# Eight x buffers, beta added ahead on GpSimd, and single groups at the end of the output stage of an attention and expert layer

## The reference

```python
x = L0_attn_X                               # 8 x 512 x 256
xn = _layernorm(x, axis=-1)
# attention
P = softmax(Q1 K1^T * s) - lam * softmax(Q2 K2^T * s)
O = P V                                     # 16 heads of 64
Y = Ocat @ Wo + bo
Yn = (Y - mean(Y)) * rsqrt(var(Y) + 1e-5) * gamma + beta
attn = Yn * (1.0 - 0.8)
# experts: each row goes to the one with the highest route probability
y = gelu(t @ w1[e] + b1[e]) @ w2[e] + b2[e]
ffn = y * route_prob_max
return x + attn + ffn
```

## Time and profile before

| | |
|---|---|
| median of 3 runs | 1817.44 us (1816.18 to 1820.64) |
| the profiled execution's own time | 1819.72 us |
| its span in the profile | 1817.9 us |
| TensorE busy | 98% |
| VectorE, ScalarE, GpSimd busy | 85%, 78%, 35% |
| granted TensorE clock, mean over the span | 0.994 of full speed |

### The profile page before, as it was taken

The page is one execution under the profiler, slowest core; times in us unless marked ns, Lnnn a source line. Parts: engine busy times, 40 slices in busy tenths (PEclk is TensorE's granted clock), DMA queues, the critical chain, the costliest instruction groups (busy, mean ns, idle before and its releaser), DMA issues. The chain is left out here.

```text
span 1817.9 us, 33121 instructions
## 1 busy us (share of the span) xinstructions
PE 1777.5 (98%) x10714; PEld 1362.8 (75%) x10714; DVE 1542.1 (85%) x2636; ACT 1423.3 (78%) x3364; POOL 639.0 (35%) x711
## 2 busy tenths in 40 slices
PE   6999999999999999999999999999999999999997
PEld 5666667777777677777777677777777689999997
DVE  4988898898889988988898889888999866887667
ACT  4998888888888888888888888888888876677622
POOL 2443222322222222222322322322226546552255
PEclk8999999999999999999999999999999999999999
DMA  8998988898889888988898898888887676667797
GB/s 245 245 252 244 246 233 227 230 248 232 224 230 245 228 226 231 249 231 225 239 239 231 221 241 241 231 221 221 224 208 200 191 263 249 238 237 259 273 368 286
DMA packets 212120, 435.05 MB, mean 239 GB/s; under 512 B 29584, under 2 KB 107152, under 8 KB 203888
## 3 DMA queue, kind: packets, MB, share of 16 engines
q1 hardware_dynamic: 207104, 418.94, 82.7%
q0 software_dynamic: 4688, 13.51, 2.3%
q10 hardware_dynamic: 160, 0.52, 0.1%
HBM read 175.17 MB, written 49.15 MB: 123 GB/s over the span
## 5 line engine op out<-in xcount | busy, mean ns | idle before, releaser
L629 ACT ACTIVATE e<-p_score,nmax 128x512 f32<-128x512 f32 x1024 | 697.2, 688 | 123.3 <-DVE nmax L976 115.7
L976 DVE TENSOR_REDUCE nmax<-p_score 128x2 f32<-128x1024 f32 x512 | 623.1, 1217 | 149.9 <-PE p_score L1135 120.6
L493 POOL TENSOR_SCALAR e<-e,rrec,lam 128x512 f32<-128x512 f32 x512 | 394.0, 769 | 977.4 <-DVE rrec L943 977.0
L1135 PE MATMUL p_score<-ks,qs 128*128 128x512 f32 x1608 | 450.1, 402 | 10.4 <-DMA ks<-k_parts 8.2
L1089 PE MATMUL p_proj<-xh,w 128*128 128x512 f32 x1024 | 386.2, 418 | 6.6 <-DVE k_parts L918 5.2
L581 ACT COPY pT<-p_tr 128x512 f32<-128x512 f32 x512 | 302.9, 592 | 104.3 <-PE p_tr L1147 98.9
L950 DVE SCALAR_TENSOR_TENSOR pm<-e,rrec 128x512 f32<-128x512 f32 x512 | 383.2, 749 | 0.4 <-POOL e L493 0.2
L1135 PEld LDWEIGHTS p_score<-ks,qs 128*128 128x128 f32 x1608 | 292.4, 189 | 85.1 <-DMA ks<-k_parts 10.4
L1147 PEld LDWEIGHTS p_tr<-consts,pm 128*128 128x128 f32 x2048 | 241.7, 140 | 104.2 <-issue 39.6
L1147 PE MATMUL p_tr<-consts,pm 128*128 128x128 f32 x2048 | 315.1, 276 | 1.4 <-ACT pT L581 1.4
L1164 PE MATMUL p_pv<-pT,v 128*64 128x512 f32 x1024 | 247.8, 605 | 0.7 <-ACT pT L581 0.7
(11 more groups left out here) (219 smaller groups left out, 2029.8 us busy)
## 6 DMA issues: line engine op xcount, KB each, us to landing
ks<-k_parts SPq DMA_DIRECT2D x510, 256.0 KB, 5.0
qs<-q_parts SPq DMA_DIRECT2D x512, 128.0 KB, 4.7
w<-weight_parts_scratch SPq DMA_DIRECT2D x56, 1024.0 KB, 10.7
w<-in_w SPq DMA_DIRECT2D x46, 1024.0 KB, 7.3
oT_parts_scratch<-oT SPq DMA_DIRECT2D x32, 512.0 KB, 6.7
op<-oT_parts_scratch SPq DMA_DIRECT2D x16, 1024.0 KB, 9.4
wv<-weight_parts_scratch SPq DMA_DIRECT2D x56, 256.0 KB, 5.5
weight_parts_scratch<-w SPq DMA_DIRECT2D x8, 1024.0 KB, 5.8
```

The costliest lines, as they stand in the source:

```text
L493: nc.gpsimd.tensor_scalar(e2, e2, rrec[:, g % 4, 1:2], lam[:, 0:1], ALU.mult, ALU.mult).then_inc(s_e2, 1)
L629: nc.scalar.activation(ex[:, g % EX, m, :], p_score[g % 2][:, m, :], ACT.Exp, bias=nmax[:, g % 2, m:m + 1], accum_out=rsum[:, g % 4, m:m + ...
L976: vec.tensor_reduce(nmax[:, g % 2, :], p_score[g % 2][:, :, :], AXX, ALU.max, negate=True).then_inc(s_max, 1)
L1135: last_op = nc.tensor.matmul(p_score[g % 2][:, m, :], qs[j][u][:, m, qt * P:(qt + 1) * P], ks[j][u][:, m, part, :], start=(part == 0), sto ...
```

## The change

`RX = 8` buffers of x instead of 4. The four new ones lie in the place of `wo`, which is free after `s_wolo`. SP loads x of groups 4 to 7 into them in the expert stage, behind its bodies 14 to 17, and in the output stage x of group n + 6 where it loaded that of n + 2. GpSimd adds beta of groups 0 to 3 behind its subtraction of tiles 8 to 11, that of 4 to 7 behind the fetches of groups 0 to 3, and that of group n + 2 behind the fetch of group n for n from 6 to 13. The groups 12 to 15 have a turn of their own each. The semaphores `s_x` stay four; SP waits for `s_xb` (beta of group n - 4 is added) before it loads x of group n.

```diff
@@ -1288,8 +1288,9 @@
-        G, R, GROUPS = 2 * P, 4, T // (2 * P)
-        OUT_TURNS = [(n, n + 1) for n in range(0, GROUPS - 2, 2)] + [(GROUPS - 2,), (GROUPS - 1,)]
+        G, R, RX, GROUPS = 2 * P, 4, 8, T // (2 * P)
+        BETA_FROM, BETAS, MORE_FROM, LATE = 8, 4, 14, 6
+        OUT_TURNS = [(n, n + 1) for n in range(0, GROUPS - R, 2)] + [(n,) for n in range(GROUPS - R, GROUPS)]
@@ -1322,6 +1323,7 @@
         x = [sb(f"x{r}", [P, 2, E]) for r in range(R)]
+        x += [wo[:, 2 * r:2 * r + 2, :] for r in range(RX - R)]
@@ -1472,8 +1474,10 @@
             def load_x(n):
                 if n >= R:
-                    sp.wait_ge(s_out, 2 * (n - R) + 2)
-                sp.dma_start(x[n % R][:, :, :], x_v[n]).then_inc(s_x[n % R], 16)
+                    sp.wait_ge(s_xb, n - R + 1)
+                if n >= RX:
+                    sp.wait_ge(s_out, 2 * (n - RX) + 2)
+                sp.dma_start(x[n % RX][:, :, :], x_v[n]).then_inc(s_x[n % R], 16)
@@ -1499,7 +1503,13 @@
-            turns(body, before_last=first_o)(sp)
+            def more_x(n):
+                if n == MORE_FROM:
+                    sp.wait_ge(s_wolo, 2)
+                if 0 <= n - MORE_FROM < RX - R:
+                    load_x(n - MORE_FROM + R)
+
+            turns(body, before_last=first_o, after=more_x)(sp)
@@ -1515,8 +1525,8 @@
                 if n >= 2:
                     store_out(n - 2)
-                    if n - 2 + R < GROUPS:
-                        load_x(n - 2 + R)
+                    if n - 2 + RX < GROUPS:
+                        load_x(n - 2 + RX)
@@ -1543,36 +1570,19 @@
-            pool.wait_ge(s_scaled, 1)
-            pool.wait_ge(s_w2lo_dve, 1)
-            add_beta(0)
-            add_beta(1)
+                if n == BETA_FROM:
+                    pool.wait_ge(s_scaled, 1)
+                if 0 <= n - BETA_FROM < BETAS:
+                    add_beta(n - BETA_FROM)
+
             pool.wait_ge(s_st[0], 16 * (LOOPED // 2 + 1))
             pool.wait_ge(s_st[1], 16 * (LOOPED // 2))
             for n in range(GROUPS):
                 fetch(n)
-                if n in (1, 2):
-                    add_beta(n + 1)
-                if n >= R:
-                    add_beta(n)
+                if n < RX - BETAS:
+                    add_beta(BETAS + n)
+                if 0 <= n - LATE < GROUPS - RX:
+                    add_beta(RX + n - LATE)
```

More of the change, by code:

```diff
@@ L1535, in gather @@
                     ahead.gather(pool, n, s)
-            for n in range(FFN_TILES):
-                if n + 2 < FFN_TILES:
-                    gather(n + 2)
-                if n == 0 or PAIR_TILES <= n < FFN_TILES - 1:
-                    continue
-                pool.wait_ge(s_w2hi, n + 1)
-                j, f = n % 2, HALF_F if n == FFN_TILES - 1 else FT
-                nc.gpsimd.tensor_tensor(w2p[j][:, 1, 0:f, :], w2[j][:, 0:f, :], w2p[j][:, 0, 0:f, :].bitcast(F32),
-                                        ALU.subtract).then_inc(s_w2lo, 1)
             def add_beta(n):
                 pool.wait_ge(s_x[n % R], 16 * (n // R + 1))
-                nc.gpsimd.tensor_tensor(x[n % R][:, :, :], x[n % R][:, :, :],
+                nc.gpsimd.tensor_tensor(x[n % RX][:, :, :], x[n % RX][:, :, :],
                                         beta.unsqueeze(1).to_broadcast([P, 2, E]), ALU.add).then_inc(s_xb, 1)
@@ L1562, in fetch @@
                     ).then_inc(s_ff[r], 16)
-            pool.wait_ge(s_scaled, 1)
-            pool.wait_ge(s_w2lo_dve, 1)
-            add_beta(0)
-            add_beta(1)
+            for n in range(FFN_TILES):
+                if n + 2 < FFN_TILES:
+                    gather(n + 2)
+                if n == 0 or PAIR_TILES <= n < FFN_TILES - 1:
+                    continue
+                pool.wait_ge(s_w2hi, n + 1)
+                j, f = n % 2, HALF_F if n == FFN_TILES - 1 else FT
+                nc.gpsimd.tensor_tensor(w2p[j][:, 1, 0:f, :], w2[j][:, 0:f, :], w2p[j][:, 0, 0:f, :].bitcast(F32),
+                                        ALU.subtract).then_inc(s_w2lo, 1)
+                if n == BETA_FROM:
+                    pool.wait_ge(s_scaled, 1)
+                if 0 <= n - BETA_FROM < BETAS:
+                    add_beta(n - BETA_FROM)
             pool.wait_ge(s_st[0], 16 * (LOOPED // 2 + 1))
@@ L1797, in base @@
                 for s in range(2):
[L1798 to L1799 removed]
+                    v.scalar_tensor_tensor(out=x[n % RX][:, s, :], in0=ff[r][s][:, :],
+                                           scalar=prob[:, 2 * n + s:2 * n + s + 1], in1=x[n % RX][:, s, :],
                                            op0=ALU.mult, op1=ALU.add).then_inc(s_base, 1)
@@ L1817, in result @@
                                            scalar=m[:, 5, 2 * k + s:2 * k + s + 1],
-                                           in1=x[r][:, s, :], op0=ALU.mult, op1=ALU.add).then_inc(s_out, 1)
+                                           in1=x[n % RX][:, s, :], op0=ALU.mult, op1=ALU.add).then_inc(s_out, 1)
             for i, groups in enumerate(OUT_TURNS):
```

2 lines of the change are left out of this document (removed).

## The result

The changed kernel took 1826.48 us, the median of 6 runs (1823.99 to 1831.5); beside them the kernel before took 1816.65 us (1816.18 to 1820.64, 6 runs). The ratio is 1.0057, with a 95% interval of 1.0044 to 1.0071. In experiment 12, the same kernel once more, it was 1824.63 against 1817.41, 1.0044 (1.0031 to 1.0057). The change costs 7 to 10 us. Forecast were 1815.9 us and a range of 1813.2 to 1819.2: wrong, and wrong in sign.

A forecast was written before the change was run, and what follows sets the result against it. The prediction took TensorE and DMA to be at their limit in the output stage, with a VectorE tail. Tail order -1.6, fetch delay and relief cancelling, and beta +0.1 gave -1.5 us: 1815.9 us, range 1813.2 to 1819.2.

The forecast's parts named there:

- Beta in the experts: Expert stage: four 1.3 us GpSimd adds fit VectorE's slack three times, miss once by 0.1: +0.1 us, bounds 0 and +5.2.
- Rival C: Expert stage: each add stalls VectorE and TensorE for its length, +3.6 us in all, 1821.0 us; chance 0.07.
- the bound of 5.2 us: Expert stage: upper bound for the beta adds, 4 x 1.3 us, if VectorE had no slack.
- The sign that the prediction gave for C: Expert stage: TensorE gaps just before bodies 10 to 13 would show that the adds stall it.
- x loads: Four x loads moved into expert turns 14 to 17: taken as 0, at most 4 x 0.65 us without spare DMA time.
- Tail order: End of output stage: single turns for groups 12 to 15 end VectorE's chain at 1813.5 against 1815.08, -1.6 us.
- Fetch delay: Start of output stage: group 4's beta between fetches 0 and 1 delays the first result by +1.15 us net.
- relief: Output stage DMA: four later bursts lose 0.25 MB of x each; bounds 0 and -1.3 us, taken as cancelling the fetch delay.
- A: Output stage: DMA relief without delay, the queue absorbs it; -2.9 us, 1814.5 us; chance 0.15.
- B: Output stage: earlier fetches 5 and 6 slow the group 6 loads; +1.2 us, 1818.7 us; chance 0.12.
- D: End of span: the last store's landing and wait set the tail, not VectorE; no change, 1817.4 us; chance 0.06.

The follow-up runs named there:

- experiment 12: The changed kernel once more, unchanged, profiled a second time: 1824.63 us against 1817.41 before, ratio 1.0044.
- run 16: Changed kernel with its four expert-stage adds of beta at half width (128 of 256 columns): 1820.11 us against 1816.38 before, ratio 1.0018.
- run 1: Changed kernel with the beta adds of groups 0 to 3 moved behind the last expert tile: 1818.96 us against 1815.94 before, ratio 1.0015.
- run 5: Changed kernel with betas 0 to 3 behind the last expert tile and the four x loads behind body 21: 1819.01 us against 1816.98 before, ratio 1.0019.
- run 13: Changed kernel with one beta add in the experts (tile 8), other three behind the last expert tile: 1817.12 us against 1816.38 before, ratio 1.0012.
- run 6: Kernel before with single turns for groups 12 to 15 and nothing else: 1817.92 us against 1816.98 before, ratio 1.0008.
- run 14: Changed kernel with two beta adds in the experts (tiles 8 and 9), other two behind the last expert tile: 1818.69 us against 1816.38, ratio 1.0008.
- run 8: Changed kernel with GpSimd's w2 subtraction waiting for VectorE's last w1 subtraction in tiles 8 to 12: 1827.86 us against 1816.98, ratio 1.0072.
- run 3: Changed kernel with the four beta adds moved to the half tiles, behind bodies 17 to 20: 1821.72 us against 1815.94 before, ratio 1.0033.

## Why the prediction was wrong, point by point

**Beta in the experts: +0.1 forecast, 8.0 and 8.9 measured in the full tiles. This is the step that failed**, in three places. It compared each add with the slack of its body as if each body began with the whole of it; but the slack ahead of TensorE went 1.50 to 0.70 and then to 0.12 us over the first two adds (VectorE's `xsp` ended at 1570.40 and 1582.97, TensorE went on at 1571.10 and 1583.09), since VectorE idles only 1.0 to 1.7 us in such a body. It priced the add at 1.3 us, and beside VectorE's subtractions it took 2.27 to 2.29; what VectorE lost by the second and the third add was 1.6 and 2.2 us (its `wo` and first `hp` subtraction took 3.47 + 1.79 and 4.03 + 1.78 us, where before they took 2.94 + 0.68 and 2.92 + 0.68). And it priced a miss by how far it misses. The deadline that counted wasn't TensorE's start but GpSimd's `w2p` subtraction: in the kernel before VectorE's last `w1p` subtraction began 1.1 us ahead of it in body 11 (1595.35 against 1596.44). Those rows of the kernel before were there to be read:

```profile
1595.35 1.21 DVE L1686 TENSOR_TENSOR w1p<-w,w1p 128x1024 fp32r<-128x1024 f32 x1
1596.44 4.64 POOL L1544 TENSOR_TENSOR w2p<-w,w2p 128x2048 fp32r<-128x2048 f32 x1 [3.86 <-ACT w2p L1615]
```

Missing it costs the rest of 4.7 us, and 1.8 to 2.7 us of lowered clock.

**Rival C** had the right engine and the right side, and a rule that held, that a held operation waits for a whole instruction. Its price was wrong in form: four times the add's own 1.3 us. Two adds cost 0.2 us in the full tiles, four cost 8 to 9. So the bound of 5.2 us, on which it rests, bounded nothing, since the longest thing that an operation can be held by is the longest instruction of the other engine, not the one that is added. The sign that the prediction gave for C, a gap of TensorE in the full tiles, came ahead of tile 12.

**x loads: 0 forecast, 0.6 to 1.5 us measured** in the half tiles of most executions, inside the 2.6 us given if the cover were gone, and 0 in run 16. The stretch that was read for their cover was of the full tiles; the half tiles, where they stand, had DMA at a share of 0.73 in the second profile of before, and 0.82 after the change (1640 to 1705).

**Tail order: -1.6 forecast, nothing measurable.** The steps came as told: in the changed profile the last turn begins 0.9 us behind TensorE's end and takes 3.47 us, without a stalled step. What failed is the base: the 9.8 us behind TensorE came from one execution, in which `low_o(15)` ended only 6.7 us ahead of TensorE's end. In the second one the tail was 7.35 us, and in both profiles of the changed kernel 7.1 to 7.2, so by that base the new order is worth 0.2 us.

**Fetch delay: +1.15 forecast for the first store, 3.3 measured** (24.63 us behind the last expert matmul, before 21.28). The term itself came out: `base` of group 1, which needs the fetched rows, began 18.54 us behind the last expert matmul, before 17.39, and that is +1.15. The other 2.2 us are VectorE beside the adds that now stand between the fetches, which the prediction priced for GpSimd alone: `base` took 1.63 us for 1.14, and a small step 1.88 for 0.17 (VectorE's row, then GpSimd's):

```profile
1740.61 1.88 DVE L1860 TENSOR_SCALAR omom<-omom 128x4 f32<-128x4 f32 x1
1741.15 1.31 POOL L1549 TENSOR_TENSOR wo<-wo,rows 128x512 f32<-128x512 f32 x1
```

The two fetches of group 1, of which the prediction said that each could stretch by 0.5 us, took 1.77 and 0.95 us. At the end the delay was worth nothing that could be seen: O is 103.2 and 101.9 against 104.8 and 101.5. That fetch delay and relief cancel is neither shown nor refuted, and rivals A, B and D can't be told apart by an O that scatters by 3 us. TensorE's gaps there were 0.37 and 0.73 us, at groups 6 and 7 and not at 10 to 12.

**Open** is 1 to 4 us. Runs 1, 5, 13 and 16 have medians 0.7 to 3.7 us above the kernel before, while their profiles leave 0 to 1.3 us in E8 and an O of 102.1 to 105.9, of which only the 2.95 us gap of run 5 has a known cause. One profile of each doesn't show it, since O alone scatters by 3 us. No version here beats the kernel before; runs 6 and 14 can't be told from it.

## What to carry to other kernels

An operation that is added to an engine with a shared port is not priced by its own length. Look for the next long instruction of the other engine, read how many microseconds lie between it and the last operation that must be ahead of it, in each body, and subtract the lateness from body to body, for idle time per body is what pays it back. Up to that margin the addition is almost free (here 0.2 us for two adds), and beyond it the price is the long instruction plus what TensorE's clock does after the pause; and before a term of 1 or 2 us is built on one profiled execution, profile the same kernel twice.

## What the runs showed of the hardware

- Only some of VectorE's operations are held by a running GpSimd instruction. At 1583.29 `y<-p_y,b`, which reads PSUM, took its 0.69 us in the middle of GpSimd's 5.73 us, and the `wo` subtraction with both inputs in SBUF that began behind it took 4.03. In run 8 a reduction, too, kept its 1.21 us inside GpSimd's 4.63:

```profile
1562.27 1.21 DVE L1769 TENSOR_REDUCE wo_mean<-wo 128x4 f32<-128x1024 f32 x1
```

```profile
1560.21 4.63 POOL L1573 TENSOR_TENSOR w2p<-w,w2p 128x2048 fp32r<-128x2048 f32 x1 [5.40 <-DVE w1p L1698]
```

- The place between held and not held is narrow: a subtraction of VectorE that by its row began 0.03 us ahead or 0.04 us behind GpSimd's kept its 1.21 us, one at 0.09 us behind took 5.57.
- A pause of 5.9 us in TensorE cost 1.8 us (7.44 for 5.67) in one execution and 2.7 in another behind it, at a granted clock of 0.50 to 0.52; in run 3 the clock fell to 0.50 behind a gap of 0.91 us, and two groups took 4.4 us more than usual together (5.36 for 2.88, 5.05 for 3.09).
- Two profiles of one kernel gave the same 161.8 us for E8 to 0.02 us, and 104.8 and 101.5 for the output stage, where DMA runs at its full share.
